# Linear attention inside a decoder layer: the values become the stationary operand, two heads share the array's columns, and denominators are inverted as exp(-ln)

## What is computed

```python
q, k, v = heads(x @ Wq), heads(x @ Wk), heads(x @ Wv)     # 16 heads of 64
q, k = elu(q) + 1, elu(k) + 1
a = sigmoid(x @ Wa + ba + 2.0)                            # decay, one per token and head
def step(carry, inp):                                     # over the tokens t
    S, z = carry
    S = a_t * S + k_t (outer) v_t
    z = a_t * z + k_t
    return (S, z), (q_t @ S) / (q_t . z + 1e-6)
x = layernorm(x + concat(out) @ Wo)
```

## Time and profile before

| | us |
|---|---|
| median of 3 runs (lowest, highest) | 1658.95 (1656.03, 1664.06) |
| the profiled execution, its own time | 1666.57 |
| its span in the trace | 1664.6 |
| linear attention, within the span | about 0 to 777 |
| cross attention | about 780 to 1100 |
| routing, experts, combine | about 1100 to 1664.6 |
| busy over the whole span: PE, DVE, ACT, POOL | 1370.5, 920.7, 873.7, 633.9 |

### The profile page before, as it was taken

One profiled execution on the slowest core, in us unless ns is written; L12 is line 12 of the kernel. 1 busy time (PEld: TensorE's weight loads), 2 busy tenths in 40 slices (PEclk: granted clock), 3 DMA queues, 4 the chain that ended last, 5 costly groups with the idle time before them and its releaser, 6 DMA issues. The chain is left out here.

```text
span 1664.6 us, 31009 instructions
## 1 busy us (share of the span) xinstructions
PE 1370.5 (82%) x10183; PEld 1203.1 (72%) x10183; DVE 920.7 (55%) x2167; ACT 873.7 (52%) x1813; POOL 633.9 (38%) x593
## 2 busy tenths in 40 slices
PE   4899999999999999997787877751699999988200
PEld 3799999999999999996555655531588888888200
DVE  3455556555555555564656566639445445456445
ACT  4665566666666655665255555520255545545335
POOL 4111111111111111113375676611376666667464
PEclk9999999999999999998888799875699999999655
DMA  3200000000000000001222232302254454555243
GB/s 120 72 14 20 13 19 19 19 19 13 19 19 13 19 19 13 14 14 32 68 61 68 67 96 67 86 32 80 67 177 155 145 171 148 156 162 168 80 120 116
DMA packets 123501, 115.69 MB, mean 70 GB/s; under 512 B 42242, under 2 KB 104298, under 8 KB 123434
## 3 DMA queue, kind: packets, MB, share of 16 engines
q1 hardware_dynamic: 116618, 96.23, 18.8%
q0 software_dynamic: 6816, 18.62, 4.2%
HBM read 83.93 MB, written 24.07 MB: 65 GB/s over the span
## 5 line engine op out<-in xcount | busy, mean ns | idle before, releaser
L298 POOL TENSOR_SCALAR_AFFINE_SELECT a_decay<-a_decay 128x256 f32<-128x256 f32 x256 | 114.1, 451 | 632.8 <-ACT a_decay L358 632.5
L467 DVE TENSOR_TENSOR a_probs<-a_ps_s,a_decay 128x384 f32<-128x384 f32 x256 | 131.8, 553 | 178.9 <-PE a_ps_o L646 161.6
L321 ACT ACTIVATE a_qk_exp<-a_ps_qk 128x512 f32<-128x512 f32 x128 | 76.6, 598 | 183.9 <-PE a_ps_qk L560 174.7
L560 PE MATMUL a_ps_qk<-a_xT_hi,a_w_hi 128*128 128x256 f32 x512 | 144.6, 282 | 4.7 <-ACT a_qk_relu L322 4.7
L560 PE MATMUL a_ps_qk<-a_xT_lo,a_w_hi 128*128 128x256 f32 x512 | 143.3, 280 | 0.0
L560 PE MATMUL a_ps_qk<-a_xT_hi,a_w_lo 128*128 128x256 f32 x512 | 142.9, 279 | 0.0
L635 PE MATMUL a_ps_s<-a_qk 64*128 64x256 f32 (+1 forms) x1024 | 132.2, 338 | 0.2
L356 ACT ACTIVATE a_decay<-a_ps_c,a_c_now 128x256 f32<-128x256 f32 x256 | 124.6, 487 | 4.7 <-PE a_ps_c L625 3.9
L460 DVE SCALAR_TENSOR_TENSOR a_qk<-a_qk_exp,a_qk_relu 128x512 f32<-128x512 f32 x128 | 88.4, 690 | 66.0 <-ACT a_qk_relu L322 66.0
L1793 ACT CAST e_hid_hi<-e_hid 128x512 fp32r<-128x512 f32 (+1 forms) x92 | 48.9, 554 | 133.8 <-PE e_ps_y L1926 88.9
L1742 POOL TENSOR_TENSOR e_gu_lo<-e_gu_raw,e_gu_hi 128x2048 fp32r<-128x2048 f32 x23 | 106.4, 4626 | 25.4 <-ACT e_gu_hi L1766 25.0
(11 more groups left out here) (290 smaller groups left out, 4289.8 us busy)
## 6 DMA issues: line engine op xcount, KB each, us to landing
e_gu_raw<-in_L_ffn_gate_w SPq DMA_DIRECT2D x23, 512.0 KB, 3.5
e_gu_raw<-in_L_ffn_up_w SPq DMA_DIRECT2D x23, 512.0 KB, 5.0
e_dn_raw<-in_L_ffn_down_w SPq DMA_DIRECT2D x23, 512.0 KB, 6.2
y_sorted<-e_y_out SPq DMA_DIRECT2D x16, 512.0 KB, 2.9
a_x_in<-in_x SPq DMA_DIRECT2D x16, 256.0 KB, 2.7
a_x_res<-in_x SPq DMA_DIRECT2D x16, 256.0 KB, 2.7
x_rows<-a_x SPq DMA_DIRECT2D x16, 256.0 KB, 2.2
b_x_in<-x_rows SPq DMA_DIRECT2D x16, 256.0 KB
```

The source lines that it names most:

```text
L298: pool.affine_select(out=d, in_=d, compare_op=ALU.is_ge, fill=0.0, base=0, pattern=[[0, 2], [1, P]], channel_multiplier=-1)\
L467: vec.tensor_tensor(probs[h][:], ps_s[h][:, 0:TRI], decay[h][:], ALU.mult)\
L560: mm = pe.matmul(out, l, r, start=(n == 0), stop=(n == len(todo) - 1))
```

## The change

- The values (128 tokens x 64 features of one head) are the stationary operand and the probabilities of all queries move past them. The two heads of a pair use columns 0 to 63 and 64 to 127 of the array and write partitions 0 to 63 and 64 to 127 of one tile, so the output has features on the partitions: `turn_o` and its two transposes go, and so does DVE's `o_norm`.
- The denominators come from products with 64 columns of ones, which write the sum of every query to all 64 partitions of its head, in the same tile (`ps_o[...][:, 1, :]`). For queries 0 to 127 they take key block 0. For queries 128 to 255 POOL first adds the two key blocks (`sum_keys`), and one product takes the sum.
- ACT computes 1/(den + 1e-6) as exp(-ln(den + 1e-6)) over 128 x 256 (`invert_den`), DVE multiplies (`normalise`, now one iteration later and first in DVE's iteration), ACT rounds, POOL takes the rest (`low_oT` moves from DVE to POOL).
- `ps_o` is double-buffered and takes the bank of `ps_t`. `weighted_values` waits for `oT_done` of two pairs before instead of `o_normed` of the pair before.
- ACT preloads one table set that has both Exp and Ln, in this stage and in `combine`.
- Two memsets of `v_aug` on POOL at the start go.

```diff
-        v_aug = [sb(f"a_v_aug{n}", [P, NB, H, DH + 1]) for n in range(2)]
+        values = [sb(f"a_values{n}", [P, NB, H, DH]) for n in range(2)]
...
-        probs = [sb(f"a_probs{h}", [P, TRI]) for h in range(2)]
-        den, rden = sb("a_den", [P, NB, 2]), sb("a_rden", [P, NB, 2])
-        o_norm = sb("a_o_norm", [P, NB, 2, DH])
+        probs, key_sum = sb("a_probs", [P, 2, TRI]), sb("a_key_sum", [P, 2, P])
+        ln_den, rden = sb("a_ln_den", [P, N]), [sb(f"a_rden{n}", [P, N]) for n in range(2)]
+        oT = [sb(f"a_oT{n}", [P, N]) for n in range(2)]
...
-        eps_col = sb("a_eps_col", [P, 1])
+        eps_col, den_eps = sb("a_eps_col", [P, 1]), sb("a_den_eps", [P, 1])
...
-        ps_o = ps("a_ps_o", [P, 512])
-        ps_t = ps("a_ps_t", [P, 512])
+        ps_o = [ps(f"a_ps_o{n}", [P, 2, N]) for n in range(2)]
         ps_y = ps("a_ps_y", [P, NB, D])
-        o_view = ps_o[:, 0:NB * 2 * (DH + 1)].rearrange("p (b h d) -> p b h d", b=NB, h=2)
...
-            for n in range(2):
-                pool.memset(v_aug[n][:], 1.0).then_inc(consts_step, 1)
             pool.memset(eps_col[:], LN_EPS).then_inc(consts_step, 1)
-            pool.wait_ge(consts_step, 7)
+            pool.wait_ge(consts_step, 5)
...
-            pool.wait_ge(consts_step, 12)
-            pool.memset(den[:], 1.0).then_inc(consts_ready, 1)
+            pool.wait_ge(consts_step, 10)
+            pool.memset(den_eps[:], EPS).then_inc(consts_ready, 1)
...
+            def sum_keys(b, g):
+
+                for h in range(2):
+                    pool.wait_ge(probs_done[h], b * PAIRS + g + 1)
+                pool.sem_inc(pool_turns, 1)
+                pool.tensor_tensor(key_sum[:], probs[:, :, P:N], probs[:, :, N:TRI], ALU.add).then_inc(keys_summed, 1)
+
+            def low_oT(b, g):
+                pool.wait_ge(oT_hi_done, b * PAIRS + g + 1)
+                pool.sem_inc(pool_turns, 1)
+                pool.tensor_tensor(oT_lo[g % 2][:], oT[g % 2][:], oT_hi[g % 2][:].bitcast(F32), ALU.subtract).then_inc(oT_lo_done, 1)
+
             def sequence(b, par):
                 for g in range(PAIRS):
                     mask_decay(b, g)
+                    sum_keys(b, g)
+                    if exists(b, g, 2):
+                        before, _, pair = back(b, par, g, 2)
+                        low_oT(before, pair)
 
             all_sequences(pool, sequence)
+            low_oT(B - 1, PAIRS - 2)
+            low_oT(B - 1, PAIRS - 1)
 
         @block.scalar
         def _(act):
+            act.preload_act_table_set("natural_log_exp_and_others")
...
-                act.copy(v_aug[par][:, blk, half * HEADS_HALF:(half + 1) * HEADS_HALF, 0:DH],
+                act.copy(values[par][:, blk, half * HEADS_HALF:(half + 1) * HEADS_HALF, :],
...
+            def invert_den(b, g):
+
+                n = b * PAIRS + g
+                act.wait_ge(o_made, n + 1)
+                act.activation(ln_den[:], ps_o[g % 2][:, 1, :], ACT.Ln, bias=den_eps[:]).then_inc(ln_done, 1)
+                act.wait_ge(ln_done, n + 1)
+                if exists(b, g, 2):
+                    act.wait_ge(oT_done, n - 1)
+                act.activation(rden[g % 2][:], ln_den[:], ACT.Exp, scale=-1.0).then_inc(rden_done, 1)
+
             def high_oT(b, g):
-                act.wait_ge(oT_made, b * PAIRS + g + 1)
-                if not isinstance(b, int) or b or g >= 2:
+                act.wait_ge(oT_done, b * PAIRS + g + 1)
+                if exists(b, g, 2):
                     act.wait_ge(y_added, b * PAIRS + g - 1)
-                act.copy(oT_hi[g % 2][:], ps_t[:, 0:NB * P]).then_inc(oT_hi_done, 1)
...
                         high_oT(before, pair)
+                    if exists(b, g, 1):
+                        before, _, pair = back(b, par, g, 1)
+                        invert_den(before, pair)
...
-            for g in (PAIRS - 2, PAIRS - 1):
-                high_oT(B - 1, g)
+            high_oT(B - 1, PAIRS - 2)
+            invert_den(B - 1, PAIRS - 1)
+            high_oT(B - 1, PAIRS - 1)
...
@@ -464,23 +495,15 @@
                 vec.wait_ge(o_made, b * PAIRS + g)
                 for h in range(2):
                     vec.wait_ge(decay_masked[h], b * PAIRS + g + 1)
-                    vec.tensor_tensor(probs[h][:], ps_s[h][:, 0:TRI], decay[h][:], ALU.mult)\
+                    vec.tensor_tensor(probs[:, h, :], ps_s[h][:, 0:TRI], decay[h][:], ALU.mult)\
                         .then_inc(probs_done[h], 1)
 
             def normalise(b, g):
                 n = b * PAIRS + g
-                vec.wait_ge(o_made, n + 1)
-                vec.tensor_scalar(den[:], o_view[:, :, :, DH], EPS, None, ALU.add).then_inc(den_step, 1)
-                vec.wait_ge(den_step, 2 * n + 1)
-                vec.reciprocal(rden[:], den[:]).then_inc(den_step, 1)
-                vec.wait_ge(den_step, 2 * n + 2)
-                vec.wait_ge(oT_made, n)
-                vec.tensor_tensor(o_norm[:], o_view[:, :, :, 0:DH],
-                                  rden[:].unsqueeze(3).to_broadcast([P, NB, 2, DH]), ALU.mult).then_inc(o_normed, 1)
-
-            def low_oT(b, g):
-                vec.wait_ge(oT_hi_done, b * PAIRS + g + 1)
-                vec.tensor_tensor(oT_lo[g % 2][:], ps_t[:, 0:NB * P], oT_hi[g % 2][:].bitcast(F32), ALU.subtract).then_inc(oT_lo_done, 1)
+                vec.wait_ge(rden_done, n + 1)
+                if exists(b, g, 2):
+                    vec.wait_ge(oT_lo_done, n - 1)
+                vec.tensor_tensor(oT[g % 2][:], ps_o[g % 2][:, 0, :], rden[g % 2][:], ALU.mult).then_inc(oT_done, 1)
...
+                    if exists(b, g, 2):
+                        before, _, pair = back(b, par, g, 2)
+                        normalise(before, pair)
                     if g == 0 or has(b, 1):
                         finish_qk(*projected_before(b, g))
                     if g == 5 and has(b, 1):
...
                     weigh(b, g)
-                    if exists(b, g, 1):
-                        before, _, pair = back(b, par, g, 1)
-                        normalise(before, pair)
-                    if exists(b, g, 2):
-                        before, _, pair = back(b, par, g, 2)
-                        low_oT(before, pair)
...
+            normalise(B - 1, PAIRS - 2)
             normalise(B - 1, PAIRS - 1)
-            low_oT(B - 1, PAIRS - 2)
-            low_oT(B - 1, PAIRS - 1)
...
             def weighted_values(b, par, g):
+                n = b * PAIRS + g
                 pe.wait_ge(v_done, VU * (b + 1))
-                pe.wait_ge(o_normed, b * PAIRS + g)
+                if exists(b, g, 2):
+                    pe.wait_ge(oT_done, n - 1)
                 for h in range(2):
-                    pe.wait_ge(probs_done[h], b * PAIRS + g + 1)
-                    v = [v_aug[par][:, j, 2 * g + h, :] for j in range(NB)]
-                    pe.matmul(o_view[:, 0, h, :], probs[h][:, 0:P], v[0], start=True, stop=True)
-                    pe.matmul(o_view[:, 1, h, :], probs[h][:, P:N], v[0], start=True, stop=False)
-                    mm = pe.matmul(o_view[:, 1, h, :], probs[h][:, N:TRI], v[1], start=False, stop=True)
+                    pe.wait_ge(probs_done[h], n + 1)
+                out = [ps_o[g % 2][h * DH:(h + 1) * DH, :, :] for h in range(2)]
+                for j, keys, cols in ((0, slice(0, N), slice(0, N)), (1, slice(N, TRI), slice(P, N))):
+                    for h in range(2):
+                        pe.matmul(out[h][:, 0, cols], values[par][:, j, 2 * g + h, :], probs[:, h, keys],
+                                  start=(j == 0), stop=(j == 1), skip_group_check=True)
+                for h in range(2):
+                    pe.matmul(out[h][:, 1, 0:P], ones[:, 0:DH], probs[:, h, 0:P], start=True, stop=True)
+                pe.wait_ge(keys_summed, n + 1)
+                for h in range(2):
+                    mm = pe.matmul(out[h][:, 1, P:N], ones[:, 0:DH], key_sum[:, h, :], start=True, stop=True)
                 mm.then_inc(o_made, 1)
...
-            def turn_o(b, g):
-                pe.wait_ge(o_normed, b * PAIRS + g + 1)
-                pe.wait_ge(oT_lo_done, b * PAIRS + g)
-                for blk in range(NB):
-                    mm = pe.transpose(ps_t[:, blk * P:(blk + 1) * P],
-                                      o_norm[:, blk, :, :].rearrange("p h d -> p (h d)"), ident[:])
-                mm.then_inc(oT_made, 1)
...
@@ -673,9 +692,6 @@
                         project_v(b + 1, g - 1, 0)
                     if exists(b, g, 1):
                         weighted_values(*back(b, par, g, 1))
-                    if exists(b, g, 2):
-                        before, _, pair = back(b, par, g, 2)
-                        turn_o(before, pair)
                     if exists(b, g, 3):
                         before, _, pair = back(b, par, g, 3)
                         add_y(before, pair)
...
             pe.wait_ge(w_lo_done, 4)
             all_sequences(pe, sequence)
             weighted_values(B - 1, (B - 1) % 2, PAIRS - 1)
```

(19 more changed lines are left out.)

## The result

The changed kernel takes 1640.66 us (median of 4 runs, 1640.53 to 1642.37) where the kernel before took 1661.20 (4 runs, 1656.03 to 1664.06) beside it: ratio 0.987, 95% interval [0.985, 0.989]. That is 21 us less, well inside the range and less than half of the 47.5 forecast. The profiled execution fell from 1666.57 to 1640.67.

The account below looks back on a forecast made before the run. PE's stream was taken to bound the linear attention's main loop. Savings of 40.5 (loop), 2.2 (last sequence), 1.3 and 1.3 (start), 0.9 (end of linear attention) and 1.3 (combine) made 47.5: 1658.95 to 1611.5 us, range 1594 to 1650.

Parts of the forecast that it names:

- The product step: PE's products of a pair in the main loop: eight products of two passes, 1.23 us with both mode changes.
- the rival of short passes: Weight loads of 128-column product passes not hidden on PE: 0.48 us lost per pair, 1715 us in all; chance 0.12.
- s: Time of a pair of product passes with 128 moving columns on PE: taken as 0.108 us, upper bound 0.245.
- ACT did not become the bound: Rival: ACT's Ln and Exp per pair make ACT set the main loop's pace, no change, 1652 us; chance 0.12.
- ACT over 85%: Sign of the rival in which ACT bounds the main loop: ACT busy over 85% of the loop.
- POOL's key sums: Two sums of about 0.5 us each added to POOL's 0.9 per pair, hidden behind PE's work.
- Loads in the old loop: ACT's table loads in the main loop before the change: taken as hidden, so removing them there gains nothing.
- PE-bound, so the loop costs what PE's stream costs: Main loop of the linear attention: PE never waits, so savings were summed on PE's passes alone.
- 119 pairs at 0.34: Pairs in iterations with projections: products to output go from 1.74 to 1.40 us each, 40.5 us saved in all.
- The start: Before the first sequence: 1.3 us saved by dropping POOL's memsets and 1.3 by removing a bare table load.
- The end of the linear attention: From last products to last output: 3.2 us, 0.4 more than before; less a table load of 1.28, net 0.9 saved.
- Combine: One table load in the chain at combine's end goes, 1.3 us saved; its other loads counted as nothing.

Follow-up runs that it names:

- e8: e1 with two more idle Ln per pair on ACT, into a tile nobody reads; ratio 0.980 to the kernel before.
- e11: The kernel before with only the change's two table-set preloads added; ratio 0.997 to the kernel before.
- e1: The changed kernel with PE's sequence loop head placed at the start of a block of 256 instructions; 1610 us, ratio 0.977 to the kernel before.
- e4: The kernel before with PE's loop head placed 208 instructions behind a block's start; ratio 1.012 to the kernel before unaltered.
- e5: e1 with the products put ahead of the value projection in two iterations of each sequence; 1602.65 us, ratio 0.972 to the kernel before.
- e12: e1 with two memsets of 3.6 us each put back in POOL's chain of constants; 1627.90 us, one run.
- e7: e1 without the table-set preload ahead of combine; ratio 0.979 to the kernel before.
- e10: The changed kernel with PE's loop head 96 instructions behind a block's start; ratio 0.980 to the kernel before.
- e13: The changed kernel with PE's loop head 104 instructions behind a block's start; 1648.9 us, one run.

## Why the prediction was wrong

**What held.** The product step: 1.24 against 1.23 forecast, with couples of 128 columns 0.11 apart (0.108 forecast). This settles the rival of short passes: s is not 0.245. The rule of the Trainium skill (TensorE: Matmul & The Clock Gate, Part 3, The mechanism) that a weight load overlaps a running matmul only in another row group does not describe these column tiles: with loads of 0.137 a couple follows the last in 0.11. ACT did not become the bound: it still waits for the projection in each iteration, and is busy 32.6 us per sequence against 33.3 forecast; e8 put 0.98 us per pair more on it nearly free. My sign for that rival, ACT over 85%, was set too low. POOL's key sums take 0.74, not 0.5, and stay hidden. Loads in the old loop were hidden (e11).

**The step that failed first** is "PE-bound, so the loop costs what PE's stream costs", read as: 119 pairs at 0.34. I counted the passes that PE streams and not the instructions that it holds, and put the loop's branch at nothing without a reason. The order of instructions had it: a pair gains two passes net (16 in place of 12 and two transposes), each a load and a matmul, so the body of two sequences grows from 1636 to 1701 instructions. With the place where its head fell (no row gives that slot), that reached too far, and five branches cost 16.9 us in the profile. e1 against the changed kernel: 0.987 against 0.977, 17 us; e4 brings the same stall to the kernel before.

**The second** is the size of 0.34. Without the stops a sequence gains 1.81, not 8 x 0.34 = 2.72; e1, where nothing stalls, gains the same. The output's first pass behind a change of mode takes 0.22 (399.67 to 399.89), not the 0.17 that I took over from full-width products, so 1.46 in place of 1.40: 8 x 0.06. And I took the 1.74 of an iteration in which products follow scores for all eight. In g = 1 and 2 they follow the value projection; there the old products needed no change of mode and took 1.28 to the turn where others took 1.39, and the new ones bring one more (0.33 to their first pass against 0.24). That is 0.20 twice, 0.4 per sequence; e5 took 0.37 of it back. The two make 0.9 of 0.91. Over the 15 sequences it is 14.2 us short. With the stops, 31.1 of the 47.5 are gone; that the profiled pair shows 25.7 all the same is owed to larger terms at both ends and, by luck, to the scatter of the stages that the change leaves alone.

**Other terms.** The start gave 5.1 in this profile, and 3.0 to 5.0 in those of the experiments on it, against 2.6. Of this 2.4, not 1.3, come from the memsets, whose chain also held up DVE (e12), which I took to be untouched by it, since I read only PE's wait for POOL; 1.25 is the table load (e11). The rest was not taken apart. The end of the linear attention: 3.1 from the last product pass (751.2) to the last output (754.30), as forecast (3.2). Combine: 0.8 to 1.6 by e7, as forecast (1.3).

With the head in place (e1) the change gives some 39 us (0.023 of 1659) of the 47.5.

## What to carry to other kernels

Count an engine's instructions in a loop's body as well as its time: before and after the change, from the head's place in a block. A few instructions more can cost a stall in every turn. Look at the branch's own duration, at idle time of the engine for "issue" behind it, and at packets of the instruction queues inside the loop; pin the head, hint the branch or unroll. Price a step in each neighbourhood that it has in the loop, since a change of mode belongs to a pair of steps and not to one.

## What the runs showed of the hardware

A backward branch of PE takes 0.21 us when the body is resident and 3.3 to 5.1 when not (e1, e4, e13). A body of 1701 instructions stays resident over whole turns with nothing fetched if it ends at 1797 from a block's start (e10), and is fetched whole, some nine packets of 16.4 kB, if at 1805 (e13). The Trainium skill (Runtime: NRT & Kernel Launch, Instruction fetch mechanics) gives PE a memory of 2048 instructions, refilled in 16 KiB blocks of 256, and warns of branches out of the window. The packets agree in size, and seven blocks plus one read ahead would make its eight; that is an inference, which no run shows. What it says of a sequential prefetch without a cache, and of a fetch whenever the target lies outside the current window of two pages, does not agree: in the kernel before and in e1 the branch goes back by 1636 and 1701 instructions, over six of its blocks, took 0.21 us, and no packet came for 440 us of loop.

Five stops of PE of 1.89 to 1.93 us stood in the changed loop. Behind four of them the granted clock fell from 1.00 (2.4 GHz) for a while, to a mean of 0.66 over 3.8 us behind the first, which cost 1.6 us more each; behind the third it stayed at 1.00.

Two operations of DVE that read and write SBUF alone took 3.1 us longer beside POOL's selects (e12), and one of the three selects took 3.86 us where it takes 2.00 in e1.
